# A hand-written order of work in the second self attention: the queries' projection set ahead of the product with the values, and the next weights' flips ahead of the rotation

## The reference, cut to what matters

```python
def _L1_attn_ref(hidden_states, w_qkv, w_o):      # hidden_states = layernorm(x), (8, 64, 512)
    HIDDEN, HQ, HKV, D = 512, 32, 4, 64
    ...
    qkv = jnp.einsum('bsh,oh->bso', hidden_states, w_qkv).reshape(b, s, HQ + 2 * HKV, D)
    q = qkv[:, :, :HQ]
    k = qkv[:, :, HQ:HQ + HKV]
    v = qkv[:, :, HQ + HKV:]
    q = _rope(q, pos)
    k = _rope(k, pos)
    k = jnp.repeat(k, rep, axis=2)                # rep = HQ // HKV = 8
    v = jnp.repeat(v, rep, axis=2)
    scores = jnp.einsum('bqhd,bkhd->bhqk', q, k) * D ** (-0.5)
    scores = jnp.where(causal[None, None], scores, jnp.finfo(scores.dtype).min)
    attn = jax.nn.softmax(scores, axis=-1)
    out = jnp.einsum('bhqk,bkhd->bqhd', attn, v).reshape(b, s, HQ * D)
    return jnp.einsum('bso,ho->bsh', out, w_o)
```

## Time and profile before

| | |
|---|---|
| median of 3 runs | 2544.89 us (2544.1 to 2547.37) |
| the profiled execution: device time | 2557.27 us |
| the profiled execution: span | 2555.5 us |
| PE, DVE, ACT, POOL busy, share of the span | 90%, 64%, 47%, 40% |
| second self attention in the span | 2146 to 2442 us, some 12% |
| mean granted PE clock over the span | 0.941 |

### The profile page before, as it was taken

How to read it: one execution, slowest core, us unless ns; L and a number is a source line. 1 busy time by engine, 2 the same in 40 slices (tenths; PEclk the granted TensorE clock), 3 DMA queues, 4 the chain that set the end, 5 groups by cost and what they waited for, 6 DMA issues and landing times. The chain is left out here.

```text
span 2555.5 us, 45882 instructions
## 1 busy us (share of the span) xinstructions
PE 2288.6 (90%) x16212; PEld 1813.5 (71%) x16212; DVE 1629.1 (64%) x2618; ACT 1206.9 (47%) x2236; POOL 1034.5 (40%) x718
## 2 busy tenths in 40 slices
PE   4799999999996999969979999999999988888766
PEld 2677777777763888857757788888888866666644
DVE  5367887777785333334422788888788864666663
ACT  2355665666542333313213676666666652233242
POOL 4168988898882000001100455455444530011320
PEclk8799999999996999979999999999999988899889
DMA  3000000001001122114230000000000011111200
GB/s 111 26 2 27 27 27 12 17 27 48 2 1 35 62 66 66 37 22 95 66 108 17 27 27 18 12 27 27 19 10 27 1 66 39 38 37 33 80 1 17
DMA packets 104280, 89.92 MB, mean 35 GB/s; under 512 B 32752, under 2 KB 82432, under 8 KB 104080
## 3 DMA queue, kind: packets, MB, share of 16 engines
q1 hardware_dynamic: 103792, 87.28, 11.3%
q0 software_dynamic: 288, 0.00, 0.0%
HBM read 86.22 MB, written 1.05 MB: 34 GB/s over the span
## 5 line engine op out<-in xcount | busy, mean ns | idle before, releaser
L2276 POOL TENSOR_TENSOR xT<-xT,x1b_ring 128x512 f32<-128x512 f32 (+1 forms) x176 | 248.4, 1411 | 212.6 <-ACT x1b_ring L2406 205.7
L941 POOL TENSOR_TENSOR x0b_krstd<-x0b_krstd,minus_half 128x24 f32<-128x24 f32 x64 | 267.5, 4180 | 88.3 <-DVE x0b_krstd L1004 84.7
L961 POOL TENSOR_TENSOR xT<-xT,x0b_ring 128x512 f32<-128x512 f32 (+1 forms) x170 | 240.3, 1413 | 40.1 <-ACT x0b_ring L1178 25.4
L111 DVE TENSOR_TENSOR x1b_plo<-x1b_ring,x1b_phi 128x512 fp32r<-128x512 f32 (+1 forms) x208 | 222.0, 1067 | 5.3 <-issue 4.7
L2421 ACT ACTIVATE x1b_ring<-x_ps,x1b_keymask 128x512 f32<-128x512 f32 (+1 forms) x208 | 143.1, 688 | 130.5 <-DVE xT L2348 125.8
L1178 ACT ACTIVATE x0b_ring<-x0b_ring 128x512 f32<-128x512 f32 (+1 forms) x208 | 131.2, 631 | 150.1 <-DVE x0b_ring L1022 141.7
L1054 DVE TENSOR_TENSOR x0b_ring<-x_ps,x0b_krstd 128x512 f32<-128x512 f32 (+1 forms) x208 | 142.8, 686 | 75.4 <-PE x_ps L846 74.3
L116 PE MATMUL x_ps<-x1b_qy,x1b_yT 128*128 128x512 f32 (+1 forms) x416 | 175.1, 421 | 4.3 <-ACT x1b_ring L2421 2.9
L2348 DVE SCALAR_TENSOR_TENSOR xT<-x_ps,x1b_keymask,xT 128x512 f32<-128x512 f32 (+1 forms) x176 | 131.2, 746 | 57.6 <-PE x_ps L118 56.7
L116 PE MATMUL x_ps<-x1b_phi,x1b_yv 128*128 128x512 f32 (+1 forms) x416 | 165.8, 399 | 1.5 <-ACT x1b_out_sb L2388 1.5
L118 PE MATMUL x_ps<-x1b_qy,x1b_yT 128*128 128x512 f32 (+1 forms) x416 | 163.9, 394 | 0.0
(11 more groups left out here) (588 smaller groups left out, 5760.5 us busy)
## 6 DMA issues: line engine op xcount, KB each, us to landing
x_y<-in_ctx_dram SPq DMA_DIRECT2D x8, 1536.0 KB
x_y<-in_ctx_dram SPq DMA_DIRECT2D x24, 512.0 KB, 3.9
a_wn<-in_L_attn_W_Q_dram SPq DMA_DIRECT2D x16, 256.0 KB, 3.1
a_wn<-in_L_attn_W_K_dram SPq DMA_DIRECT2D x16, 256.0 KB, 3.4
a_wn<-in_L_attn_W_V_dram SPq DMA_DIRECT2D x16, 256.0 KB, 4.0
a_won<-in_L_attn_W_O_dram SPq DMA_DIRECT2D x16, 256.0 KB, 2.8
x1a_wq<-in_L_xattn_Wq_dram SPq DMA_DIRECT2D x4, 1024.0 KB, 10.6
x1c_wo<-in_L_xattn_Wo_dram SPq DMA_DIRECT2D x8, 512.0 KB, 6.9
```

What stands on the lines that cost most here:

```text
L111: return v.tensor_tensor(lo, exact, hi.bitcast(F32), ALU.subtract)
L941: ins = g_.tensor_tensor(r, r, c.minus_half[:, 0:8].unsqueeze(1).broadcast_to([P, whole, 8]), ALU.pow)
L961: g_.tensor_tensor(total[half][0:m, :], old, src, ALU.add).then_inc(summed, 1)
L2276: g_.tensor_tensor(total[half][0:m, :], old, src, ALU.add).then_inc(summed, 1)
```

## The change

The four texts of letters get another order. Q comes before V; W comes before R. In the head's line C comes after both. The prologue and the body's extra `V Q` follow. Nothing is computed otherwise, and no instruction is added or taken away.

```diff
-        HEAD = "N R1 R0 W O F0 F1 G S V C Q"
-        INNER = "N R0 W O F0 F1 G S V Q"
-        TAIL = "N R0 W A0 O F0 F1 G A1 S"
+        HEAD = "N W R1 R0 O F0 F1 G S Q V C"
+        INNER = "N W R0 O F0 F1 G S Q V"
+        TAIL = "N W R0 A0 O F0 F1 G A1 S"
...
             if part == "prologue":
-                return (window(1, "A0 A1 W") + window(2, "B") + window(1, "Q") + window(2, "R1 R0 W G S C Q")
-                        + window(3, "N R0 W G F0 F1 S V Q"))
+                return (window(1, "A0 A1 W") + window(2, "B") + window(1, "Q") + window(2, "W R1 R0 G S C Q")
+                        + window(3, "N W R0 F0 F1 G S Q V"))
             if part == "body":
-                return (window(0, INNER) + window(1, TAIL) + window(2, "B") + window(1, "V Q") + window(2, HEAD)
+                return (window(0, INNER) + window(1, TAIL) + window(2, "B") + window(1, "Q V") + window(2, HEAD)
                         + window(3, INNER))
             return (window(0, INNER) + window(1, "N R0 O F0 F1 G S V") + window(2, "N O F0 F1 V")
                     + window(3, "O"))
```

## The result

| | before | changed |
|---|---|---|
| median of 6 runs each | 2548.37 us (2544.10 to 2563.88) | 2559.34 us (2555.98 to 2563.82) |
| changed to before | | 1.0040, interval 1.0021 to 1.0060 |
| the profiled execution | 2557.27 us | 2557.45 us |
| first L to last L in it | 242.04 us | 242.58 us |

The change makes the kernel 0.4% slower. The forecast was 2548.4 us with a range of 2538 to 2558, so the time lies outside it. The two profiled executions are level, though, in time and in the stage. That is the riddle of this case: the executions of before spread over some 20 us, and the profiled one, which is none of the six, is among its long ones.

A forecast was written before the change was run, and what follows sets the result against it. It took a chain through DVE, ACT and PE, with PE's clock, as the bound. Full-clock terms of -6.8 us and +10 for clock falls made about +3.5: 2560.8 against the profile, 2548.4 us as median, range 2538 to 2558.

The forecast's parts named there:

- 3-0: Step from L to L where R waits for ACT: 14.3 us, one loss of 0.4, three gains of 0.9 to 1.0, sum -2.4.
- 1-2: Step from L to L set by DVE's chain through two rotations: 17.7 us against 16.28, +1.4 each, +4.2 in all.
- The clock in the new order: Falls behind new PE gaps ahead of S: 7.7 us in steps 0-1 and 1-2, 2.5 in chain-bound steps, together +10, bounds 0 to 17.
- 2-3: Step from L to L set by PE: R's wait of 0.82 gets covered, 15.0 left of 15.86, -2.5 us in all.
- 0-1: Step from L to L where S will wait for G's low part: 16.0 us, -4.3 for three; the last one 13.6, -2.6.
- -6.8: Sum in us at full clock of the terms for all four kinds of steps and the prologue's +0.8.
- I carry the difference over: The runs' median lies 12.4 us under the profiled execution, so 2560.8 us for the new profile became 2548.4.
- The clock falls everywhere: Rival: falls at S behind DVE's chain in 1-2 and 0-1, eight at 2.3 us, +11 net, 2556 us; chance 0.22.
- The clock stays up: Rival: the new, shorter gaps keep the clock at 1.00 but for one or two falls, -5 to -7, 2539 us; chance 0.18.
- the chain is shorter: Rival: W's low part and V's copy cost less, ten chain-bound steps lose 0.5 each, -5 more, 2543 us; chance 0.10.
- Nothing earlier: Rival: something else holds R, so only the +4.2 of 1-2 stays, about +4 us; chance 0.05.
- The ports of DVE and POOL: Shared port lock: by the rule POOL's moved product holds nothing; otherwise 0.56 us a step, 6 us in all.

The follow-up runs named there:

- e6: Changed kernel with matmuls of zeros added in PE's new gaps to hold the clock up: 2551.84 us, ratio to before 1.0003.
- e2: Changed kernel run again, unaltered: 2562.15 us, ratio to before 1.0039.
- e1: Kernel before, run again without any change: 2549.75 us, ratio 0.9993; its profiled execution took 2547.72 us.
- e11: Changed kernel with matmuls of zeros, POOL's cosine product cut from 512 to 64 columns in loop and last part (output incomplete): 2550.08 us, ratio to before 0.9997.
- e5: Kernel before with matmuls of zeros added on PE ahead of R and S to hold the clock up: 2546.13 us, ratio to before 0.9983.
- the mix: Kernel before with W ahead of R in 0-1 and the change's order in 2-3 only: 2545.75 us; with matmuls of zeros 2546.79 us.

## Why the prediction was wrong

*The arithmetic of the new steps was right.* At the full clock it said 14.3, 16.0, 17.7 and 15.0, together 63.0. Measured with the clock held (e6): 14.72, 15.91, 17.54 and 14.93, together 63.1. The pieces hold too: R in 3-0 at L+5.67 as worked out, with a wait of 1.57; in 1-2 the copy of V at L+6.77 (said 6.85), `crossed` at L+12.40 (12.40), `qT` at L+15.35 (15.37), S waiting 2.48 (2.6).

*One term was mis-sized, 3-0.* It said 14.3 and took 14.7. I took the step from V's low part to N from the earlier trace rows, which is 1-2, where it is 0.84. In 3-0 the loop turns in between, and it is 1.35. Another 0.1 is W's low part to `crossed`, 1.02 and not 0.92. V's copy, at L+5.69 and not 5.75, gives a little back, and so does the end: from `qT` to the next L it is 2.15 and not 2.33. Steps 3-0 in the loop lose 0.9 against before at the full clock, not the 0.4 of the text.

*The clock in the new order had the right sum, and half of it at the right place.* S behind the gap of 2.48 in 1-2 was followed by a clock under 1.00 in three of three places, and 2-3 paid for it: 16.5 instead of 14.9, together 4.7 (the term had 3.8 for these steps). In e2 two of the three were: behind the first of these gaps S and the whole 2-3 ran at 1.00. But the three steps 0-1 of the loop, given as much again, paid nothing in the first profile (15.92 each, as with the clock held). The rest was at the start of the stage, in the 3-0 and in the last 0-1 (14.64 against 13.39). +10 us was the term; the changed kernel without the Z is 7.5 us (2559.34) to 10.3 us (2562.15) over the one with them, and some 9 by the ratios. That the sum fits is in part luck.

*The step that failed is the baseline.* "-6.8" compares new steps at the full clock with old steps as the first profile had them, and that profile is an execution of 2557.27 us whose falls lay at bad places. Against before at the full clock (3-0 13.8, 0-1 15.6, the last 13.3) the profiled steps were some 12.9 us too long: 3-0 59.65 for four against 55.16, 0-1 52.27 for three against 46.81, the last 16.20 against 13.27. So the same order of steps that "gained" 6.8 costs +6.1; measured with the clock held in the loop, 5.7. And then the text took the 12.4 us between profile and median off again ("I carry the difference over"). But e1 shows what that difference is: an execution near the median has a stage 12.8 us shorter. The 12.4 were the falls that had already been taken off as gains. They were counted twice. Before at about 2546 with the clock held, plus 6.1, plus 10, is 2562; the runs gave 2559 and 2562. The text's own 2560.8, ahead of the carrying over, was the better forecast. The stage of e1 was 12.8 shorter and its whole 9.6: it came to its first L 4.3 us later (2181.64 against 2177.32), and behind the last L it was 1.1 shorter.

The median of before moved as well: 2544.89 in three runs, 2548.37 in six, 2551.53 in the 35 beside e2. The first of these steps is 3.5 of the 10.9 us by which the forecast was low; the change itself was forecast at +3.5 and came to +11.0.

The warning was in sight: the three runs lay within 3.3 us, and the profiled one 10 above the highest of them. A profile that far out had to differ from them somewhere, and the earlier trace rows showed where, in 3-0 and 0-1 of uneven lengths beside 1-2 and 2-3 of even ones.

*The rivals.* "The clock falls everywhere" named a right place, S in 1-2 with 2-3 paying, but also 0-1, where nothing was paid in the loop; it gave 2556, from the same wrong baseline. "The clock stays up" was wrong, "the chain is shorter" too. "Nothing earlier" was wrong: R did come 0.5 earlier. The "gains of 0.9, 0.9, 1.0" in 3-0 were the trap: in e1 the same kernel does not pay for those waits.

*The ports of DVE and POOL.* It was predicted that POOL's product would hold nothing, and e11 shows that this was right: a product of an eighth of the length left 3-0 at 14.72. (That POOL has its rotation alone in this stretch was misread for the last step 0-1, where the next stage's POOL work already runs, 9.80 us busy in the earlier trace rows.)

## What to carry to other kernels

Before a change is summed against a profile, ask whether that execution is a typical one: where steps of one kind differ among themselves, take the shortest as the baseline (neighbours together, since the short 2-3 of e1 stands behind a long 1-2), book the rest as the clock's, and carry a difference between profile and median over only if no term has used it. In a pipeline with several kinds of steps, pick the order for each kind by itself: the same two letters gain about 0.8 us where PE is full (2-3) and cost 1.0 where they put twelve matmuls ahead of the result that the slowest chain waits for (1-2). And work out what stands between two instructions of a queue at that very place, a loop's turn included.

## What the runs showed of the hardware

- A turn of the loop costs DVE 0.5 us between two instructions (0.65 and 0.63 against 0.15; 0.16 when it is written out), entering the loop 0.2 (0.35), leaving it 0.15 (0.31).
- The same code has executions with the clock at 1.2 GHz behind the wait ahead of R in most steps 3-0 and 0-1 and others with none: 242.04 and 229.26 us for the same stage, with the same idle time ahead of R (2.64 and 2.61). The length of one gap does not say whether the clock falls. Matmuls of zeros in the gaps shrank the scatter of 12 runs from 17 us to 6 (before), from 11 to 8 (changed) and from 19 to 12 (the mix).
- A stretch of 10.2 us at 0.50 met most profiles once from the first S on, and PE was busy nearly all through it (in e5 10.24 of 10.24, from 2237.81 on). Behind a wait of 3.8 us or more it came in seven of seven profiles, behind one of 2.16 in four of six. No run here shows its cause.
